# The feed-forward's first pair of row tiles is combined and transposed inside the attention's last two slots

## The reference, cut to what matters

```python
x = layernorm(x + attn(x))                  # autocorrelation attention: softmax over top lags
x = layernorm(x + xattn(ctx, ctx, x))       # 16 batches of 256 rows x 2048
x = layernorm(x + ffn(x))                   # x @ W_base.T + mixture of rank-8 experts
# xattn: sim = einsum(ctx, x) / 16; softmax; context = sim @ ctx
# ffn:   out = x @ W_base.T + sum over the two best of 8 experts of (x @ A.T) * weight @ B.T
```

## Time and profile before

| | us |
|---|---|
| median of 3 runs | 1961.65 |
| profiled execution, its own time | 1965.13 |
| its span, first to last instruction | 1963.3 |
| PE busy | 1781.1 (91%) |
| DVE busy | 1362.4 (69%) |
| ACT busy | 791.5 (40%) |
| POOL busy | 200.3 (10%) |
| DMA, mean rate over the span | 241 GB/s |

### The profile page before, as it was taken

How to read it: one execution, slowest core, us unless ns; L and a number is a source line. 1 busy time by engine, 2 the same in 40 slices (tenths; PEclk the granted TensorE clock), 3 DMA queues, 4 the chain that set the end, 5 groups by cost and what they waited for, 6 DMA issues and landing times. The chain is left out here.

```text
span 1963.3 us, 27039 instructions
## 1 busy us (share of the span) xinstructions
PE 1781.1 (91%) x10210; PEld 952.8 (49%) x10210; DVE 1362.4 (69%) x2607; ACT 791.5 (40%) x939; POOL 200.3 (10%) x362
## 2 busy tenths in 40 slices
PE   3989999999853959999999999997899999999997
PEld 2666666666531425444544444543344444444443
DVE  3888788888759856677766677789655565465553
ACT  5888888788735221222222222234221222122111
POOL 1223232323200000000000000000010010001000
PEclk8999999999975989999999999999999999999999
DMA  8899999999759499999999999955999888988883
GB/s 279 203 290 260 295 240 291 261 290 245 222 192 245 110 237 252 257 258 237 249 251 262 249 239 221 239 173 161 264 257 266 269 238 253 258 261 224 266 249 118
DMA packets 565595, 472.70 MB, mean 241 GB/s; under 512 B 498448, under 2 KB 502544, under 8 KB 544656
## 3 DMA queue, kind: packets, MB, share of 16 engines
q1 hardware_dynamic: 565456, 470.87, 88.0%
HBM read 237.51 MB, written 109.58 MB: 177 GB/s over the span
## 5 line engine op out<-in xcount | busy, mean ns | idle before, releaser
L1578 PE MATMUL bank_f<-w_hi_f,a_cols_f 128*128 128x512 f16 x3584 | 1091.9, 382 | 78.8 <-DMA a_cols_f<-rows_f 62.7
L1578 PE MATMUL bank_f<-w_lo_f,a_cols_f 128*128 128x512 f16 x1792 | 684.8, 382 | 0.0
L1578 PEld LDWEIGHTS bank_f<-w_hi_f,a_cols_f 128*128 128x128 f16 x3584 | 351.6, 98 | 509.5 <-DVE w_lo_f L1305 40.8
L1157 ACT ACTIVATE rows_f<-xn_f 128x1024 f16<-128x1024 f32 x78 | 82.4, 1056 | 506.2 <-DMA xn_f<-x_scratch 341.4
L1578 PEld LDWEIGHTS bank_f<-w_lo_f,a_cols_f 128*128 128x128 f16 x1792 | 175.8, 98 | 204.6 <-issue 3.3
L1336 DVE SCALAR_TENSOR_TENSOR y_f<-bank_f,w_iscale_f,y_f 128x512 f32<-128x512 f32 x192 | 134.6, 743 | 169.6 <-PE bank_f L1578 169.1
L649 PE MATMUL ps_s_fast<-k_both_fast,q_hi_fast 128*128 128x256 f16 x1024 | 169.9, 274 | 7.7 <-DMA k_both_fast<-v_lo_fast 6.8
L1297 DVE TENSOR_TENSOR rows_f<-xn_f,rows_f 128x1024 f16<-128x1024 f32 x78 | 94.5, 1211 | 101.7 <-ACT rows_f L1157 101.6
L1297 DVE TENSOR_TENSOR rows_f<-sums_f,rows_f 128x1024 f16<-128x1024 f32 x63 | 77.0, 1222 | 119.7 <-ACT rows_f L1157 119.6
L1336 DVE SCALAR_TENSOR_TENSOR y_f<-bank_f,w_iscale,y_f 128x512 f32<-128x512 f32 x192 | 134.9, 745 | 29.4 <-PE bank_f L1578 25.0
L1157 ACT ACTIVATE rows_f<-sums_f 128x1024 f16<-128x1024 f32 x63 | 66.3, 1053 | 194.3 <-DMA a_cols_f<-rows_f 191.8
(11 more groups left out here) (215 smaller groups left out, 2261.7 us busy)
## 6 DMA issues: line engine op xcount, KB each, us to landing
xbuf_fast<-x SPq DMA_DIRECT2D x32, 1024.0 KB, 7.7
x_scratch<-x2buf_fast SPq DMA_DIRECT2D x32, 1024.0 KB, 6.2
y_f<-x_scratch SPq DMA_DIRECT2D x32, 1024.0 KB, 7.7
xn_f<-x_scratch SPq DMA_DIRECT2D x62, 512.0 KB, 4.9
kept_scratch<-a_cols_f SPq DMA_DIRECT2D x45, 512.0 KB, 3.4
xn<-x_scratch SPq DMA_DIRECT2D x45, 512.0 KB, 7.0
a_cols_f<-kept_scratch SPq DMA_DIRECT2D x45, 512.0 KB, 8.9
cbuf<-ctx_in SPq DMA_DIRECT2D x16, 1024.0 KB, 6.0
```

The source lines that it names most:

```text
L1157: nc.scalar.activation(rows[g % 2][:, 0], source(i), ACT.Copy).then_inc(a_hi, 1)
L1578: ins = nc.tensor.matmul(bank[i][:], a_cols[:, i, part + kk, :], ww[:, W_SLOT[i], kk, :], start=(kk == 0 and part == 0 and ww is w_hi), st ...
```

## The change

The seven operands of pair 0 (which are batch 0, long stored) are formed in the attention's slots 14 and 15, stored to HBM (`first_items`) and loaded ready-made by the feed-forward. In slot 14 SP loads x2's batch 0 into the two context buffers (2 loads of 1 MB). GpSimd makes the five sums (`first_sum`): operands 2, 3 and 4 ahead of its `norm2(14, 0)`, operands 5 and 6 once the softmax is done. ACT makes the high parts (`first_high`) and DVE the low parts (`first_low`). SP transposes each (`turn_first`) and stores it (`store_first`, 0.5 MB each). In slot 15 the turns 3 to 6 stand ahead of the store of x2's batch 14. The prefetch of `xn0` goes. `ag_raw` and `cbuf0` are loaded after the last low part; the block's end now also waits for the seven stores.

In the feed-forward DVE loses seven `low_rows` and five `combine`, ACT seven `high_rows`, SP seven `turn` and three `keep` for pair 0. SP's order is now: unit 1, seven loads of 0.5 MB of the operands, unit 2, two blocks of pair 1, unit 3, `b_rows`, units 4 and 5, the residual, units 6 and 7. PE's first product waits for all seven loads.

SP, in `attention_pass`:

```diff
+                def load_first():
+                    for r in (1, 0):
+                        sp.wait_ge(vlo_done, R * (nb - 1) + r + 1)
+                        sp.wait_ge(stored[0][r], 16 * (base + 1))
+                        sp.dma_start(cbuf[r][:], x2_out[r * P:(r + 1) * P, :]).then_inc(c_loaded[r], 16)
+                def turn_first(i):
+                    sp.wait_ge(f_lo, i + 1)
+                    if i == NM - 1:
+                        sp.wait_ge(fwd_done, 4 * nb)
+                    elif i >= 2:
+                        sp.wait_ge(sim_done, R * nb)
+                        sp.wait_ge(folded, R * nb)
+                    sp.dma_start_transpose(f_cols[i], f_rows[i % 4].rearrange("p a c -> p (a c)")).then_inc(f_turned[i % 2], 16)
+                def store_first(i):
+                    sp.wait_ge(f_turned[i % 2], 16 * (i // 2 + 1))
+                    sp.dma_start(first_items[i], f_cols[i]).then_inc(f_stored, 16)
                 def slot(n, half, parity):
+                    if n == nb - 2:
+                        load_first()
+                    if n == nb - 1:
+                        for i in range(3, NM):
+                            turn_first(i)
+                            store_first(i - 1)
...
                         store(n - 1, 1 - parity)
...
+                    if n == nb - 2:
+                        turn_first(0)
+                        turn_first(1)
+                        store_first(0)
+                        turn_first(2)
+                        store_first(1)
+                    if n == nb - 1:
+                        store_first(NM - 1)
                 batch_slots(sp, None, nb, slot, 0)
-                sp.wait_ge(stored[0][0], 16)
-                sp.wait_ge(w_squared, 2 * W_TILES)
-                sp.dma_start(consts["xn0"][:], x2_out[0:P, :]).then_inc(prefetched, 16)
                 sp.wait_ge(fwd_done, 4 * nb)
+                sp.wait_ge(f_lo, NM)
                 sp.dma_start(consts["ag_raw"][:], ag_in.rearrange("p k c -> p (k c)")).then_inc(tables_loaded, 16)
                 sp.dma_start(consts["cbuf0"][:], w_chunks[0]).then_inc(tables_loaded, 16)
                 store(nb - 1, (nb - 1) % 2)
+                sp.wait_ge(tables_loaded, 16 * 4)
+                sp.wait_ge(f_stored, 16 * NM)
```

GpSimd, in `slot(n)`:

```diff
+                    def first_sum(i):
+                        one, two, op = OPERANDS[i]
+                        for b in (one, two):
+                            f_loaded(pool, b)
+                        if i == 2:
+                            pool.wait_ge(w_squared, 2 * W_TILES)
+                        else:
+                            pool.wait_ge(f_sum, i - 2)
+                        if i >= 5:
+                            pool.wait_ge(f_lo, 1 if i == 5 else 3)
+                            pool.wait_ge(p_ready, R * nb)
+                        g.tensor_tensor(f_source(i), f_block(one), f_block(two), op).then_inc(f_sum, 1)
                     if is_batch(n - 1, nb):
                         norm2(n - 1, 1 - parity, 1)
+                    if n == nb - 2:
+                        for i in (2, 3, 4):
+                            first_sum(i)
                     if cur and n < nb - 1:
                         norm2(n, parity, 0)
...
+                    if n == nb - 2:
+                        first_sum(5)
+                        first_sum(6)
```

ACT, in `slot(n)`:

```diff
+                    def first_high(i):
+                        if i < 2:
+                            f_loaded(act, (A22, A11)[i])
+                        else:
+                            act.wait_ge(f_sum, i - 1)
+                        if i == 0:
+                            act.wait_ge(sim_done, R * (nb - 1))
+                        if i >= 4:
+                            act.wait_ge(f_turned[i % 2], 16 * (i // 2 - 1))
+                        nc.scalar.activation(f_rows[i % 4][:, 0], f_source(i), ACT.Copy).then_inc(f_hi, 1)
+                        if n == nb - 2 and j in (5, 6):
+                            first_high(j - 5)
+                        if n == nb - 1 and j in (2, 3):
+                            first_high(j + 3)
...
                     normalise1(0)
+                    first_highs(2, 3)
                     softmax_exp(0)
...
                     guard_squares(3)
+                    first_highs(4)
```

DVE, in `slot(n)`:

```diff
+                    def first_low(i):
+                        dve.wait_ge(f_hi, i + 1)
+                        v.tensor_tensor(f_rows[i % 4][:, 1], f_source(i), f_rows[i % 4][:, 0], ALU.subtract).then_inc(f_lo, 1)
                     for j in range(CG):
                         emptied_bank(j)
+                        if n == nb - 1 and j in (4, 6):
+                            first_low(NM - 2 if j == 4 else NM - 1)
...
+                    first_lows(0, 1)
                     softmax_max(0)
...
                     softmax_norm(0)
+                    first_lows(2)
                     softmax_max(1)
+                    first_lows(3)
                     value_low(1)
                     softmax_norm(1)
+                    first_lows(4)
```

`feed_forward`, SP:

```diff
                 wait_stored(sp, x2_stored, NP_)
-                load_block(0, A22)
-                load_block(0, A21)
                 load_unit(1)
+                for i in range(NM):
+                    sp.dma_start(whole(i), first_items[i]).then_inc(kept_loaded[0], 16)
                 load_unit(2)
-                turn(0, 0)
-                turn(0, 1)
...
                 for b in (A22, A21):
                     load_block(1, b)
+                load_unit(3)
+                load_b(0)
+                load_unit(4)
                 load_unit(5)
-                turn(0, 6)
-                load_b(0)
                 load_residual(0)
                 load_unit(6)
-                keep(0, 4)
-                keep(0, 5)
                 load_unit(7)
```

`feed_forward`, PE:

```diff
                 def wait_slot(s, i):
+                    if s == 0:
+                        pe.wait_ge(kept_loaded[0], 16 * NM)
+                        return
```

More of the change, by code:

```diff
@@ L50 @@
 HALF = L // 2
+A11, A12, A21, A22 = range(4)
+OPERANDS = [(A22,), (A11,), (A21, A11, ALU.subtract), (A21, A22, ALU.add), (A12, A22, ALU.subtract), (A11, A22, ALU.add),
+            (A11, A12, ALU.add)]
+KEPT = (4, 5, 6)
 def after(eng, sem, value):
@@ L154, in attention_pass @@
         ones = sb("ones", [P, P], F32)
+        k_free = k_both[nb % 2][:].rearrange("p k t c -> p (k t c)")
+        f_rows = [k_free[:, i * L:(i + 1) * L].rearrange("p (a c) -> p a c", a=2) for i in range(4)]
+        f_spare = fwd[:].bitcast(F16).rearrange("p a c -> p (a c)")[:, 0:L].rearrange("p (k c) -> p k c", c=P)
+        f_sums = [consts["xn0"][:, 0:HALF], consts["xn0"][:, HALF:L]]
+        f_cols = [sb(f"f_cols{i}", [P, KT, P], F16)[:] for i in range(2)] + [q[:, :, i * P:(i + 1) * P] for q in (q_lo, q_hi) for i in range(2)] + [f_spare]
         w_sumsq = sb("w_sumsq", [P, 2 * (L // P + 1)], F32)
@@ L192, in attention_pass @@
         dve_step, pool_step = sem("dve_step"), sem("pool_step")
[L193 removed]
+        w_loaded, w_squared, w_summed = sem("w_loaded"), sem("w_squared"), sem("w_summed")
+        f_hi, f_lo, f_sum = sem("f_hi"), sem("f_lo"), sem("f_sum")
+        f_turned, f_stored = [sem(f"f_turned{i}") for i in range(2)], sem("f_stored")
         mv1_ready, mean2_ready, ssq2_ready, mv1_free = sem("mv1_ready"), sem("mean2_ready"), sem("ssq2_ready"), sem("mv1_free")
@@ L398, in normalise2, with first_highs @@
                                              scale=rs2[:, r:r + 1]).then_inc(x2_ready, 1)
+                    def first_high(i):
[8 more added lines that the diff above has]
+                        nc.scalar.activation(f_rows[i % 4][:, 0], f_source(i), ACT.Copy).then_inc(f_hi, 1)
+                    def first_highs(*which):
+                        if n == nb - 2:
+                            for i in which:
+                                first_high(i)
                     for j in range(CG):
@@ L492, in slot @@
                             if b == 0:
-                                after(dve, stored[parity][r], 16 * half)
+                                after(dve, stored[parity][r], 16 * (base + half))
                             dve.wait_ge(context_done, CG * n + j + 1)
@@ L908, in wait_x @@
         def wait_x(eng, s, b):
-            after(eng, x_loaded[b], 16 * (made(s) + (b // 2)))
+            after(eng, x_loaded[b], 16 * made(s))
         def wait_unit_loaded(eng, u):
@@ L1935, in decoder_layer @@
         setup(nc, consts)
-        stored, stored_again = stored_sems("fast"), stored_sems("full")
-        attention_pass(nc, x, ctx_in, x2, w_chunks, b_rows, ag_in, consts, stored, EPS4_AT, "fast")
+        kept_scratch = nc.dram_tensor("kept_scratch", (rows // (2 * P), len(KEPT), P, KT * P), F16, kind="Internal").ap()
+        first_scratch = nc.dram_tensor("first_scratch", (KEPT[0], P, KT * P), F16, kind="Internal").ap()
+        first_items = [first_scratch[i] if i < KEPT[0] else kept_scratch[0][KEPT.index(i)] for i in range(len(OPERANDS))]
```

(2 more changed lines are left out.)

83 lines of the change are left out of this document (31 added, 52 removed).

## The result

| | before | changed |
|---|---|---|
| median of 7 runs each | 1964.02 us (1959.75 to 1968.40) | 1970.05 us (1968.19 to 1972.01) |
| ratio | | 1.0027, 95% interval 1.0018 to 1.0036 |
| span of the profiled execution | 1963.3 us | 1966.4 us |
| its own time | 1965.13 us | 1968.19 us |

The changed kernel is slower, by 5.3 us (0.0027 of 1964.02; the interval is 3.5 to 7.1). The prediction had 2.8 us less.

The account below looks back on a forecast made before the run. The seam was taken to be bound by the feed-forward's start, DVE's work to unit 7, and 7.6 us. Start 12.5 later minus 15.3 saved gives -2.8, 1961.65 to 1958.9, rounded 1959; own range 1955.5 to 1962, overall 1952.5 to 1967.

Parts of the forecast that it names:

- What bounds the kernel: At the seam: time is the feed-forward's start, plus DVE's work up to unit 7, plus 7.6 us.
- The feed-forward's part: From the feed-forward's start to step 1: 13.6 + 5.6 - 4.4 + 0.5 = 15.3 us less.
- The third store: Store of operand 6 in the crowded stretch after unit 7: its removal saves 0.5 us, 1.3 at most.
- the rival in which they crawl: SP's queue ahead of unit 2: slow operand loads, at 250 GB/s +4.5 us, 1966; chance 0.15.
- The attention's part: Slots 14 and 15: 6.9 MB queue from about 571, so the feed-forward starts 12.5 us later, at 590.3.
- DMA had been idle: Before x2's last stores: SP had only the first weight chunk at 559.88 and little else, DMA idle.
- the signs named for being wrong: At the feed-forward: wrong if the start moves by less than 9 us or DVE waits over 8 for unit 2.
- The collisions: GpSimd sums against DVE low parts, slots 14 and 15: waits up to 2.4 us at three places, within pauses.
- PE's 10.57 ahead of `transposed_h`: Feed-forward, PE ready some 10 us before `transposed_h`: clock may halve, costing 0 to 2 us, taken as 0.
- DMA at its best rate: Operand loads and last stores at 439 GB/s: stall 1.7, start 11.1 later, -6.9 us, 1954.7; chance 0.25.
- GpSimd dear: GpSimd sums in slots 14 and 15 at 3.5 us each: result -0.1, 1961.6, with collisions up to 1964; chance 0.10.
- The block's end as the bound: Block's end waits for `cbuf0`, then flag and branch: start 592.3, result -0.8, late landings +2, 1963.7; chance 0.08.

Follow-up runs that it names:

- experiments 1 to 4: Edits of the changed kernel: operands 3 to 6 not turned, 1.0003; batch 14's half stored early, 1.0014; norm2 ahead of sums, 1.0026; operands 3 to 6 not stored, 0.9983.
- second pair of profiles: The kernel before and the changed kernel, each unedited and profiled again; the executions' own times were 1968.04 and 1967.47 us.
- experiment 3: Changed kernel with batch 14's norm2 ahead of GpSimd's sums and the exponential ahead of high parts 2 and 3; ratio to before 1.0026.
- three_of_seven: Changed kernel with only operands 0 to 2 formed in the attention, batch 14's first half stored in slot 14, some loads fetched earlier; ratio to before 0.9959.
- five: Changed kernel with only operands 0 to 4 formed in the attention, batch 14's first half stored in slot 14, some loads fetched earlier; ratio to before 1.0003.
- no_turns_3_6: Changed kernel with operands 3 to 6 of pair 0 stored without being transposed, values wrong; ratio to before 1.0003.
- Four operands: Changed kernel with only operands 0 to 3 formed in the attention, batch 14's first half stored in slot 14, some loads fetched earlier; ratio to before 0.9968.

## Why the prediction was wrong

**What bounds the kernel** held. Start, DVE's work up to unit 7 and 7.6 was the right sum: step 1 stood 7.5 behind unit 7's end, and what experiments 1 to 4 gained in the start came out at step 1 within 0.5.

**The feed-forward's part** held: 16.7 and, in the second pair of profiles, 85.7 - 70.0 = 15.7 less, predicted 15.3. Its terms: 12 x 1.13 = 13.6 of arithmetic, 0.55 and 5.08 of waits gone (4.42 for PE's scores in the second profile of the kernel before), 2.89 for unit 2 where I took 4.4. The third store, taken at 0.5, shows as 0.1 to 0.3 at step 1. The loads of operands ran at 383 GB/s in the window of 600 to 610, so the rival in which they crawl did not happen.

**The attention's part was the step that failed: "12.5 us later" measured 19.3 (19.1 in the second pair).** By its own steps, all from slot 14's first copy:

- Low part 6 ended 42.33 behind it (568.14 + 1.22 - 527.03), predicted 41.3: 1.1 late. This is GpSimd's and the softmax's share, which I put at 0 with bounds of 0 and 2. The softmax was late by 1.95 where I had 0.5, and low part 2 with it, so that turn 2 left DMA time unused (experiment 3).
- Turn 6 was issued 2.3 after that low part, since turn 5 held SP until 570.93 and operand 4's store until 571.58. I had given the turns no time on SP. One of them holds it for 4.3 to 4.4 while earlier transfers still flow. The trace of the kernel before had such rows, this one at pair 0's last operand:

```profile
621.72 4.32 SPq L956 DMA_TRANSPOSE a_cols_f<-rows_f  x1
```

- Turn 6 landed in 6.4, not 5.3: 1.1.
- From its landing (578.07) to the start 21.0 passed; I had 18.7. The bytes were right, 6.9 MB, but not the rate: from 578 to 596.7 6.9 MB in 18.7 us are 0.37 MB/us against my 0.41, which is 1.9 us, and 0.4 is the rest.

Together 1.1 + 2.3 + 1.1 + 2.3 = 6.8, and 12.5 + 6.8 = 19.3. Behind most of this stands one omission: I let the queue of 6.9 MB begin where turn 6 lands, which was right, but asked only when the arithmetic lets turn 6 go, and not what SP and the DMA engines can do before it. From 560 to 578 they were full with the turns and the operands' stores, at 202 to 216 GB/s, little more than half the rate of the copies behind them. I read the earlier trace rows as the transpose's latency, which it is; what counts in a row of four is occupancy. A turn and the store beside it are issued 5.1 to 5.5 us apart (561.09, 566.55, 571.67); of 5.1, 0.52 MB of store take 1.3 at 0.41 MB/us, which leaves some 3.8 for the turn, an estimate. With 19.3 - 16.7 the sum would have been +2.6, and step 1 was measured at +2.5 and +3.0.

Two things on the prediction's own signs. "DMA had been idle" holds only up to 560: the earlier trace rows has a share of 0.93 from 560 to 570. And neither of the signs named for being wrong came, a start that moves by less than 9 or a wait of over 8 for unit 2; none was named for a start that moves by more than 14.

**The small terms.** A sum on GpSimd took 2.35 to 2.36 where I took 2.4. By the Trainium skill (GPSIMD Engine Reference, "Elementwise — side-by-side cycle accounting") it was an estimated 2.25, and the trace agrees within 5%. One took 3.44: it started 0.01 behind low part 4. The collisions that I put at up to 2.4 cost 2.17 at low part 0 (3.39 instead of 1.22). PE's 10.57 ahead of `transposed_h` cost nothing, as I had taken it.

**The rivals.** DMA at its best rate fell: the copies made 358 GB/s from 580 to 590, and unit 2 still waited 2.89. GpSimd dear fell as to the price of a sum, 2.36; the collisions and the late softmax were real, and beyond the 0.75 of experiment 3 their price is estimated (some 3 us) and not measured. The block's end as the bound fell: the start stands 2.4 after the end of the data at 596.7. None of my rivals said what happened, x2's stores waiting behind turns that fill SP and the DMA engines, though I had written that they "stand behind turns 3 to 6".

**What stays open.** The seam accounts for 2.5 to 3.0 of the 5.3 us that the ratio gives. In every run the timed difference lies 1.7 to 4.1 us above what step 1 shows against the mean of the two profiles before (three operands: -9.8 at step 1, 0.0041 x 1965.26 = -8.1 timed; five: -1.7 and +0.6; `no_turns_3_6`: -3.6 and +0.6). The profiled executions' own times differ by 1967.83 - 1966.59 = 1.2 only, the two before lie 1.1 and 2.8 above their medians (1964.02 and 1965.26) and the two changed 1.9 and 2.6 below theirs (1970.05), so the profiled executions are not the middle ones; which part of the rest is real was not found. Nor do the runs separate the two things that a turn does, hold SP and fill the DMA engines, since every edit removes or adds both.

**The version that beats both** is `three_of_seven`: 1958.11 us, 8 us less than the kernel before (interval 5.5 to 10.4) and some 13 less than the changed kernel by their ratios. Four operands are as good within the measurement.

## What to carry to other kernels

When work is moved ahead into a stretch where "DMA is idle", count how long each transfer occupies its queue and the DMA engines, not only when its data is ready and how long it takes to land; here a transpose of 0.5 MB occupied them for an estimated 3.8 us, a copy of its size for 1.3. Then ask what stands behind it: here the last stores that everything waits for. Move only as much as fits ahead of them: three of seven operands gave more than half of the whole gain (9.5 of 16.7) at no cost, and the next four ate it up.

## What the runs showed of the hardware that was not expected

- Transposes of [128 x 2048] fp16 in a row, with 0.5 MB stores between them, keep the DMA share at 0.96 to 0.98 at 202 to 216 GB/s. The Trainium skill (DMA: Bandwidth & Descriptors, "Latency and other measured facts") gives a transpose 261 GB/s effective with a non-contiguous middle dimension and about 350 to 400 in the contiguous case. The windows here show less than either, though they count stores too, and here they decide.
- The issue of a transpose holds SP for 1.8 us with nothing in flight (turn 2) and for 4.3 to 4.4 behind other transfers (turns 4 to 6).
- A DVE operation on one column with two operands in SBUF (`g_lags`, 561.52) took 1.03 us where it took 0.23 in the kernel before, and ended 0.02 after a GpSimd sum (560.18 + 2.35 = 562.53, 561.52 + 1.03 = 562.55). The collision of the earlier trace rows reaches the smallest operations too.
